# Gated scan chained to the convolution by 16 turns instead of 19, in a twelve-sublayer decoder kernel

## Chip, core and metric

The kernel runs on one core of one Trainium2 chip. The metric is the device time of one launch in microseconds. The three runs of the kernel before gave 3713.7, 3722.3 and 3728.1 us, median 3722.31. The profiled execution is another run.

## What is computed

A decoder of four layers with three sublayers each, every sublayer followed by a residual sum and a layer norm: `x = layernorm(x + f(x))`. x is 128 sequences of 64 positions and 128 features in float32 (8192 tokens). Two neighbouring sublayers matter here, the third of layer 2 and the first of layer 3:

```python
def L2_ffn(x):                         # "convolution with experts"
    xc = causal_depthwise_conv(x, 3 taps) + dw_bias
    x1 = x + silu(xc @ pw_w.T + pw_b)
    logits = x1 @ router_w.T + router_b              # 8 experts, top 2, softmax over the two
    ye = silu(einsum(x1, expert_w) + expert_b)       # all 8 experts
    h = rmsnorm(x1 + (sum_e rw_e * ye_e) @ out_w.T + out_b) * norm_w
    return h + gelu(h @ ff_down_w.T + ff_down_b) @ ff_up_w.T + ff_up_b

def L3_attn(x):                        # "gated scan"
    xn = x / max(|x|, 1e-12) * sqrt(128) * gamma
    q, kv, a = split(xn @ W_qkva.T, 3);  a = sigmoid(a)
    h[t] = a[t] * h[t-1] + kv[t]                     # along the 64 positions
    return q * h
```

## The kernel before

Both x (token rows, `x_tok`) and its transpose (`x_T`) stay on chip through the whole kernel. A sublayer works on 16 chunks of 512 tokens (4 tiles of 128). The engines are programmed by hand, each with its own instruction order, and meet at semaphores.

Sublayers 9 and 10 of the list are chained (`chained`, L1933): one block runs both. On every engine the function `staged` (L1905) goes through turns i = -5, -4, ...; in each turn it calls the stages of the convolution in a fixed order and then those of the scan. A stage with lag l works on chunk i - l, if there is such a chunk. For the scan's stages the offset, 19, is added to the lag. So in turn i TensorE does, in this order, for the convolution: down product (chunk i-4), transposes of the combined experts (i-1), pointwise product, router, experts (i+1), transposes of h (i-3), the z product (i-2), up product (i-5), transposes of the normalised rows (i-7); and then for the scan: `turn_out` (lag 1), `project` (lag -1), `turn_rows` (lag -2), `turn_normed` (lag 3). ScalarE does GELU (i-4), normalise_z (i-3), copy_combined (i-1), copy_h (i-3), square (i-2), normalise (i-6), copy_transposed (i-7), and then scale_rows (-3), sigmoid (-1), copy_turned (-2), normalise_act (2), copy_transposed (3). VectorE does its routing, `combine` (i), `mean_square` (i-2), `residual` (i-5), and then the scan's `residual` (1), `scan` (0), `sum_squares` (-4). GpSimd does squares, powers and sums beside them. An instruction that waits holds up all that stands behind it on its engine.

The eight banks of PSUM all belong to the convolution: pw, route, experts0, experts1, turned, z, down_ps, up_ps. The scan takes them over as they come free. In `project` (L2367) three products of 512 columns are made for a chunk: gate a, then kv, then q. Before, a goes to route, q to experts0 or z, and kv to experts1 or down_ps, by the chunk's parity; the transposed output goes to up_ps, the transposed rows to turned. `scan` (L2442) reads the gate (sigmoid of a, in SBUF) and kv's bank, then multiplies by q's bank into `out_T`, semaphore out_done. `project(c)` waits for the sigmoid of chunk c-1 and for out_done of chunk c-2:

```python
def project(c):                       # L2367
    pe.wait_ge(xs_copied, c + 1)
    if c >= 1:
        pe.wait_ge(gated, c)
    if c >= 2:
        pe.wait_ge(out_done, c - 1)
```

RowTail (L554) is the layer norm of both: the sum and its moments on VectorE, the inverse deviation on GpSimd, normalisation on ScalarE, transposes on TensorE (L637), a copy into x_T on ScalarE (L644). Its row buffer has two places: the residual of chunk c waits until chunk c-2 is normalised (`tail.normed`, L2460). In the profile the digits of names are left out: L2_ffn is L_ffn, L3_attn is L_attn; PSUM banks keep the convolution's names in the scan too. After the scan's last copy a barrier follows, and then the attention "full".

Of the kernel before, what the change touches and what calls it, by code (L numbers as in the profile page):

```python
# [16 lines left out]
N_SUBLAYERS = tuple(range(1, 13))  # L17

ALU = mybir.AluOpType
ACT = mybir.ActivationFunctionType  # L20
# [7 lines left out]
B, S, D = 128, 64, 128  # L28
# [4 lines left out]
CHUNKS = TOKENS // CHUNK  # L33
# [277 lines left out]
class Sublayer:  # L311
# [25 lines left out]
    def bank(self, what):  # L337
        return self.ctx.enter_context(self.nc.psum_tensor(f"{self.name}_{what}", [128, 512], F32))
# [1985 lines left out]
def gated_scan(net, final, name):  # L2324
# [5 lines left out]
    before = yield  # L2330
    with ExitStack() as ctx:
# [8 lines left out]
        if before:  # L2340
            xs_bank, a_bank = before.part["pw"], before.part["route"]
            q_bank, kv_bank = [before.part["experts0"], before.part["z"]], [before.part["experts1"], before.part["down_ps"]]
            y_bank, xT_bank = before.part["up_ps"], before.part["turned"]
        else:
            xs_bank, a_bank = bank("xsT"), bank("a")
            q_bank, kv_bank = [bank("q0"), bank("q1")], [bank("kv0"), bank("kv1")]
            y_bank, xT_bank = bank("y"), bank("xT")
        rooted = sem("gamma_rooted")
# [7 lines left out]
        def tensor(pe):  # L2356
            def turn_rows(c):
                if before and c == 0:
                    pe.wait_ge(before.part["pw_done"], CHUNKS)
                pe.wait_ge(scaled, c + 1)  # L2360
                if c >= 1:
                    pe.wait_ge(xs_copied, c)
                for k in range(PER):
                    last = pe.transpose(xs_bank[:, TILE * k:TILE * k + TILE], xs[:, c % 2, k, :], net.ident[:, :])
                last.then_inc(xs_turned, 1)
# [4 lines that stand above are left out]
                    pe.wait_ge(gated, c)  # L2370
                if c >= 2:
                    pe.wait_ge(out_done, c - 1)
                if c == 0:
                    sub.await_weights(pe)
                if before and c == 0:
                    pe.wait_ge(before.part["r_steps"], before.part["n_steps"]["logits", CHUNKS - 1])
                    pe.wait_ge(before.part["expert_done"], 2 * TILES)
                if before and c == 1:
                    pe.wait_ge(before.part["squared"], CHUNKS)
                    pe.wait_ge(before.part["zn_done"], CHUNKS)  # L2380
                    pe.wait_ge(before.part["down_done"], CHUNKS)
                for r, b in ((2, a_bank), (1, kv_bank[c % 2]), (0, q_bank[c % 2])):
                    pe.matmul(b[:, :], w_s[:, D * r:D * r + D], xn_T[:, c % 2, :], start=True, stop=True)\
                        .then_inc(projected, 1)

            def turn_out(c):
                pe.wait_ge(out_done, c + 1)
                if c >= 1:
                    pe.wait_ge(tail.summed, c)
                if before and c == 0:  # L2390
                    pe.wait_ge(before.tail.summed, CHUNKS)
                for k in range(PER):
                    last = pe.transpose(y_bank[:, D * k:D * k + D], out[:, c % 2, TILE * k:TILE * k + TILE], net.ident[:, :])
                last.then_inc(y_ready, 1)

            def turn_normed(c):
                if before and c == 0 and not final:
                    pe.wait_ge(before.tail.xT_copied, CHUNKS)
                tail.transpose(pe, c, xT_bank)

            return [(1, turn_out), (-1, project), (-2, turn_rows), (3, turn_normed)]

        def scalar(act):
# [19 lines left out]
            def sigmoid(c):  # L2423
                act.wait_ge(projected, 3 * c + 1)
                if c >= 2:
                    act.wait_ge(scanned, c - 1)
                act.activation(gate[:, c % 2, :], a_bank[:, :], ACT.Sigmoid).then_inc(gated, 1)

# [3 lines left out]
        def vector(dve):  # L2432
# [9 lines left out]
            def scan(c):  # L2442
# [4 lines left out]
                dve.wait_ge(projected, 3 * c + 2)  # L2447
                dve.tensor_tensor_scan(h[:, p, :], gate[:, p, :], kv_bank[p][:, :], 0.0, ALU.mult, ALU.add)\
# [5 lines left out]
                dve.tensor_tensor(out[:, p, :], q_bank[p][:, :], h[:, p, :], ALU.mult).then_inc(out_done, 1)  # L2454

# [390 lines left out]
def conv_moe(net, final, name):  # L2846
# [30 lines left out]
    before = yield  # L2877
    with ExitStack() as ctx:
# [333 lines left out]
        def gpsimd(pool):  # L3212
# [43 lines left out]
            "z": z_bank, "down_ps": down_bank, "up_ps": up_bank, "pw_done": pw_done, "r_steps": r_steps, "n_steps": n_steps,  # L3256
            "expert_done": expert_done, "squared": squared, "zn_done": zn_done, "down_done": down_done})

# [37 lines left out]
def build_program(nc, dram):  # L3296
    with ExitStack() as ctx:
# [39 lines left out]
        def run(n, final):  # L3337
# [105 lines left out]
```

## Time and profile before

| | us |
|---|---|
| profiled execution | 3718.39 |
| its span | 3716.7 |
| median of the three runs | 3722.31 |
| TensorE busy | 2948.5 (79% of the span) |
| VectorE busy | 2177.6 (59%) |
| ScalarE busy | 1822.5 (49%) |
| GpSimd busy | 1823.2 (49%) |

Times within the profile are microseconds from the start of the span. The chained stage runs from about 2600 to 3038 us. Busy shares are averages over stages with different limits, and TensorE's clock is granted at one of two levels, so a busy TensorE may be one at half clock (0.50 in the column for the clock).

### The profile page before, as it was taken

The numbers are of one execution on the slowest core, as the hardware profiler recorded it, in microseconds if no ns is written. First come the engines' busy times: TensorE is split into PE (matmuls) and PEld (weight loads), VectorE is DVE, ScalarE is ACT, GpSimd is POOL, SyncE is SP. The second block draws the span as 40 slices with busy tenths as digits, with TensorE's granted clock in tenths as the row PEclk, the third lists the DMA queues.
The fourth block names the chain that finished last, engine by engine and source line by source line (L and its number), as shares of the span: only waits on it lengthen the run. The fifth ranks groups of instructions, "written<-read, shape, count | busy, mean of one in ns | idle before, by whom it ended". The sixth has DMA issues, their size and how long they took to land. (4 is left out here: it accounts for less than half of the span.)

```text
span 3716.7 us, 83881 instructions
## 1 busy us (share of the span) xinstructions
PE 2948.5 (79%) x28814; PEld 2037.6 (55%) x28814; DVE 2177.6 (59%) x5986; ACT 1822.5 (49%) x3516; POOL 1823.2 (49%) x1735
## 2 busy tenths in 40 slices
PE   2687873998888789963529997996999879995884
PEld 1576762775555556642316664664444546664773
DVE  2111133756888668863247886777898668883124
ACT  0233331844555556621216665775466666661332
POOL 3533264434777645526455554663133655553325
PEclk9988986999998889985559998997999789996997
DMA  8555652120010121114621112221000012213664
GB/s 282 160 180 168 193 164 68 45 8 25 32 43 37 41 74 69 71 46 127 168 54 44 55 54 87 87 85 54 1 1 1 4 26 66 73 62 107 198 204 135
DMA packets 325001, 315.46 MB, mean 85 GB/s; under 512 B 111316, under 2 KB 244854, under 8 KB 324473
## 3 DMA queue, kind: packets, MB, share of 16 engines
q1 hardware_dynamic: 283080, 261.98, 23.0%
q0 software_dynamic: 16384, 33.59, 3.0%
q10 hardware_dynamic: 25264, 16.40, 1.5%
q8 instruction: 154, 2.52, 0.3%
q14 instruction: 119, 0.97, 0.1%
HBM read 167.28 MB, written 60.69 MB: 61 GB/s over the span
## 5 line engine op out<-in xcount | busy, mean ns | idle before, releaser
L1099 ACT ACTIVATE moe_first_hid<-moe_first_hid_ps,moe_first_expert_w 128x256 f32<-128x256 f32 x340 | 139.1, 471 | 253.8 <-PE moe_first_hid_ps L1044 132.7
L1055 PE MATMUL moe_first_out_ps<-moe_first_expert_w,moe_first_hid 128*128 128x128 f32 x1360 | 203.0, 304 | 69.0 <-ACT moe_first_hid L1099 45.6
L908 DVE TENSOR_TENSOR moe_first_tile_y<-moe_first_out_ps,moe_first_expert_w 128x256 f32<-128x256 f32 x85 | 36.1, 424 | 374.2 <-PE moe_first_out_ps L1055 213.7
L1055 PEld LDWEIGHTS moe_first_out_ps<-moe_first_expert_w,moe_first_hid 128*128 128x128 f32 x1360 | 184.7, 209 | 81.7 <-issue 39.9
L1118 POOL DMA_INDIRECT slot_x<-x_tok,moe_first_slots x128 | 124.3, 971 | 121.2 <-DMA slot_x<-blank 50.0
L1044 PE MATMUL moe_first_hid_ps<-moe_first_tile_xT,moe_first_expert_w 128*128 128x256 f32 x680 | 174.1, 402 | 2.5 <-issue 1.9
L1132 POOL DMA_INDIRECT moe_first_token_y<-slot_y,moe_first_slots x128 | 123.1, 962 | 107.1 <-issue 66.4
L1814 POOL TENSOR_TENSOR causal_k_blocks<-causal_k_T,headmask 128x1024 f32<-128x1024 f32 x64 | 121.2, 1896 | 99.6 <-PE causal_scores L1424 93.8
L1814 POOL TENSOR_TENSOR alibi_k_blocks<-alibi_k_T,headmask 128x1024 f32<-128x1024 f32 x64 | 121.2, 1896 | 94.2 <-PE alibi_scores L1424 90.1
L1814 POOL TENSOR_TENSOR full_k_blocks<-full_k_T,headmask 128x1024 f32<-128x1024 f32 x64 | 120.7, 1896 | 83.9 <-PE full_scores L1424 78.9
L1099 ACT ACTIVATE moe_last_hid<-moe_last_hid_ps,moe_last_expert_w 128x256 f32<-128x256 f32 x212 | 86.7, 471 | 146.9 <-PE moe_last_hid_ps L1044 110.9
L3072 PE MATMUL L_ffn_experts<-weights_odd,x_T 128*128 128x512 f32 x256 | 145.5, 651 | 1.3 <-ACT L_ffn_expert_out L3168 1.3
L1044 PEld LDWEIGHTS moe_first_hid_ps<-moe_first_tile_xT,moe_first_expert_w 128*128 128x128 f32 x680 | 132.8, 206 | 19.7 <-issue 3.2
L1814 POOL TENSOR_TENSOR keys_k_blocks<-keys_k_T,headmask 128x1024 f32<-128x1024 f32 x64 | 120.9, 1899 | 45.8 <-PE keys_scores L1424 42.1
L908 DVE TENSOR_TENSOR moe_last_tile_y<-moe_last_out_ps,moe_last_expert_w 128x256 f32<-128x256 f32 x53 | 22.5, 424 | 193.1 <-PE moe_last_out_ps L1055 151.2
L2997 DVE SCALAR_TENSOR_TENSOR L_ffn_combined<-L_ffn_expert_out,L_ffn_mix,L_ffn_combined 128x128 f32<-128x128 f32 x448 | 128.7, 350 | 4.0
L1055 PE MATMUL moe_last_out_ps<-moe_last_expert_w,moe_last_hid 128*128 128x128 f32 x848 | 120.9, 296 | 10.4 <-ACT moe_last_hid L1099 7.5
L1814 POOL TENSOR_TENSOR diff_k_blocks<-diff_k_T,headmask 128x1024 f32<-128x1024 f32 x64 | 121.4, 1909 | 10.0 <-POOL diff_k_T L1801 5.6
L3233 POOL TENSOR_SCALAR L_ffn_ms_eps<-L_ffn_ms 128x4 f32<-128x4 f32 x16 | 3.7, 230 | 243.6 <-DVE L_ffn_ms L3005 243.6
L1055 PEld LDWEIGHTS moe_last_out_ps<-moe_last_expert_w,moe_last_hid 128*128 128x128 f32 x848 | 110.9, 203 | 16.4 <-DVE moe_last_tile_y L908 6.3
L1671 DVE TENSOR_REDUCE keys_maxima<-keys_scores 128x8 f32<-128x512 f32 x128 | 87.7, 685 | 49.6 <-PE keys_scores L1424 48.6
L1568 ACT ACTIVATE diff_probs_T<-diff_pT 128x512 f32<-128x512 f32 x128 | 76.1, 595 | 78.9 <-PE diff_pT L1438 78.5
(561 smaller groups left out, 8931.2 us busy)
## 6 DMA issues: line engine op xcount, KB each, us to landing
moe_first_expert_w<-in_L_attn_experts SPq DMA_DIRECT2D x85, 578.0 KB
moe_last_expert_w<-in_L_ffn_experts SPq DMA_DIRECT2D x53, 578.0 KB
moe_first_tile_x<-slot_x SPq DMA_DIRECT2D x85, 128.0 KB
slot_y<-moe_first_tile_y SPq DMA_DIRECT2D x85, 128.0 KB
slot_x<-blank ACTq DMA_DIRECT2D x2, 4992.0 KB, 36.5
L_ffn_tile_x<-slot_x SPq DMA_DIRECT2D x32, 256.0 KB
slot_y<-L_ffn_tile_y SPq DMA_DIRECT2D x32, 256.0 KB
moe_last_tile_x<-slot_x SPq DMA_DIRECT2D x53, 128.0 KB
```

The source lines that it names most:

```text
L908: dve.tensor_tensor(y_out[:, q, :, :], out_bank[q][:, 0:SLOT_TILE].rearrange("p (s d) -> p s d", s=SPAN), over(wall[:, j % RING, 2 * FF + ...
L1044: last = pe.matmul(hid_bank[h][:, SLOT_TILE * (b % 2):SLOT_TILE * (b % 2) + SLOT_TILE], wall[:, j % RING, 128 * b:128 * b + 128], xT[:, j ...
L1055: last = pe.matmul(out_bank[j % 2][:, D * s:D * s + D], hid[:, j % 2, b, TILE * s:TILE * s + TILE], wall[:, j % RING, FF + D * b:FF + D * ...
L1099: act.activation(hid[:, j % 2, b, :], hid_bank[b // 2][:, SLOT_TILE * (b % 2):SLOT_TILE * (b % 2) + SLOT_TILE], gelu, bias=wall[:, j % RIN ...
L1118: pool.indirect_dma_start(slot_x[part][:, :], bass.IndirectOffsetOnAxis(slots[:, part, r, t:t + 1], 0), net.x_tok[:, origin[part] + t, :], ...
L1132: pool.indirect_dma_start(y_in[:, p, k, r, :], None, slot_y[part][0:NTS[part] * SLOT_TILE, :], bass.IndirectOffsetOnAxis(slots[:, part, r, ...
L1568: act.activation(probs_T[:, t.p, 4 * g:4 * g + 4, :].rearrange("p k t -> p (k t)"), pT_bank[:, :], ACT.Copy)\
L1671: dve.tensor_reduce(maxima[:, t.p, heads], src, AX_X, ALU.max).then_inc(max_done, 1)
L1814: pool.tensor_tensor(k_blocks[:, t.p, :, :], keys.to_broadcast([128, 8, TILE]), lanes.to_broadcast([128, 8, TILE]), ALU.mult).then_inc(spr ...
L2997: last = dve.scalar_tensor_tensor(combined[:, p, k, :], expert_out[:, p, k, e, :], w, combined[:, p, k, :], ALU.mult, ALU.add)
L3072: pe.matmul(expert_bank[g][:, :], net.x_T[:, TILE * t:TILE * t + TILE], experts_s[:, 4 * g:4 * g + 4, :].rearrange("p e d -> p (e d)"), st ...
L3233: pool.tensor_scalar(ms_eps[:, :], ms[:, :], 1.0 / D, 1e-6, ALU.mult, ALU.add).then_inc(ms_eps_done, 1)
```

## The change

The offset is 16. The banks are assigned anew: the gate goes to experts0 for chunks 0 to 4 and to down_ps after, q to experts0 (from chunk 6 on odd chunks to up_ps), kv to experts1 (from chunk 8 on odd chunks to turned), the transposed output to route, the transposed rows to z. Where a chunk's q or kv bank is that of the chunk before, `project` waits for out_done of the chunk before; where the gate and q share a bank, the q product waits for the sigmoid. The waits for the convolution's last use of each bank move to the chunk that first takes it.

```diff
         if before:
-            xs_bank, a_bank = before.part["pw"], before.part["route"]
-            q_bank, kv_bank = [before.part["experts0"], before.part["z"]], [before.part["experts1"], before.part["down_ps"]]
-            y_bank, xT_bank = before.part["up_ps"], before.part["turned"]
+            xs_bank, y_bank, xT_bank = before.part["pw"], before.part["route"], before.part["z"]
+            a_banks = [before.part["experts0"] if c < 5 else before.part["down_ps"] for c in range(CHUNKS)]
+            q_banks = [before.part["up_ps"] if c % 2 and c >= 6 else before.part["experts0"] for c in range(CHUNKS)]
+            kv_banks = [before.part["turned"] if c % 2 and c >= 8 else before.part["experts1"] for c in range(CHUNKS)]
...
                 if c >= 2:
                     pe.wait_ge(out_done, c - 1)
+                if c >= 1 and (q_banks[c] is q_banks[c - 1] or kv_banks[c] is kv_banks[c - 1]):
+                    pe.wait_ge(out_done, c)
                 if c == 0:
                     sub.await_weights(pe)
                 if before and c == 0:
-                    pe.wait_ge(before.part["r_steps"], before.part["n_steps"]["logits", CHUNKS - 1])
                     pe.wait_ge(before.part["expert_done"], 2 * TILES)
-                if before and c == 1:
-                    pe.wait_ge(before.part["squared"], CHUNKS)
-                    pe.wait_ge(before.part["zn_done"], CHUNKS)
+                if before and c == 5:
                     pe.wait_ge(before.part["down_done"], CHUNKS)
-                for r, b in ((2, a_bank), (1, kv_bank[c % 2]), (0, q_bank[c % 2])):
-                    pe.matmul(b[:, :], w_s[:, D * r:D * r + D], xn_T[:, c % 2, :], start=True, stop=True)\
-                        .then_inc(projected, 1)
+                if before and c == 7:
+                    pe.wait_ge(before.tail.summed, CHUNKS)
+                if before and c == 9:
+                    pe.wait_ge(before.part["combT_copied"], CHUNKS)
+                    pe.wait_ge(before.part["hT_copied"], CHUNKS)
+                    pe.wait_ge(before.tail.xT_copied, CHUNKS)
+                pe.matmul(a_banks[c][:, :], w_s[:, 2 * D:3 * D], xn_T[:, c % 2, :], start=True, stop=True).then_inc(projected, 1)
+                pe.matmul(kv_banks[c][:, :], w_s[:, D:2 * D], xn_T[:, c % 2, :], start=True, stop=True).then_inc(projected, 1)
+                if a_banks[c] is q_banks[c]:
+                    pe.wait_ge(gated, c + 1)
+                pe.matmul(q_banks[c][:, :], w_s[:, 0:D], xn_T[:, c % 2, :], start=True, stop=True).then_inc(projected, 1)
...
                 if before and c == 0:
-                    pe.wait_ge(before.tail.summed, CHUNKS)
+                    pe.wait_ge(before.part["r_steps"], before.part["n_steps"]["logits", CHUNKS - 1])
...
                 if before and c == 0 and not final:
-                    pe.wait_ge(before.tail.xT_copied, CHUNKS)
+                    pe.wait_ge(before.part["squared"], CHUNKS)
+                    pe.wait_ge(before.part["zn_done"], CHUNKS)
...
-                return chained(net, [conv_moe(net, False, "L2_ffn"), gated_scan(net, N_SUBLAYERS[-1] == 10, "L3_attn")], 19)
+                return chained(net, [conv_moe(net, False, "L2_ffn"), gated_scan(net, N_SUBLAYERS[-1] == 10, "L3_attn")], 16)
```

## Rows read from the trace of the kernel before

**Rows 1.** Windows: length, busy us (instructions) of each engine, TensorE's granted clock, DMA.

```profile
core 0: us, PE busy (x) PEld busy (x) DVE busy (x) ACT busy (x) POOL busy (x), PEclk, DMA share, GB/s
2892.50:2895.00 2.50, 0.25 (x3) 0.28 (x4) 2.46 (x4) 2.15 (x6) 2.42 (x3) 1.00 0.00 0
2895.00:2905.00 10.00, 10.00 (x40) 8.13 (x38) 9.79 (x30) 2.82 (x6) 1.31 (x2) 0.51 0.00 0
...
2895.00:2940.00 45.00, 40.18 (x147) 28.16 (x145) 18.80 (x64) 19.89 (x50) 24.18 (x33) 0.58 0.00 1
...
2953.20:3024.10 70.90, 57.04 (x248) 32.97 (x248) 63.73 (x198) 61.57 (x151) 47.85 (x82) 1.00 0.04 6
```

**Rows 2.** Groups by line, VectorE, 2960 to 3010: count, busy us, mean ns, idle before.

```profile
L580 DVE BATCH_NORM_STATS2 L_attn_ln_stats<-L_attn_resid_sum 128x6 f32<-128x128 f32 x40 | 8.7, 281 | 0.3
...
L2461 DVE TENSOR_TENSOR L_attn_resid_sum<-L_ffn_up_ps,x_tok 128x512 f32<-128x512 f32 x10 | 6.9, 692 | 2.7 <-ACT x_tok L612 2.5
...
L2435 DVE TENSOR_REDUCE L_attn_ss<-L_attn_sq 128x4 f32<-128x512 f32 x10 | 6.7, 674 | 0.0
...
L2448 DVE TENSOR_TENSOR_SCAN L_attn_h<-L_attn_gate,L_ffn_down_ps 128x512 f32<-128x512 f32 x5 | 6.1, 1221 | 0.2
...
L584 DVE BATCH_NORM_AGGREGATE L_attn_ln_moments<-L_attn_ln_stats 128x2 f32<-128x6 f32 x40 | 3.8, 157 | 0.3
...
L2454 DVE TENSOR_TENSOR L_attn_out_T<-L_ffn_z,L_attn_h 128x512 f32<-128x512 f32 x5 | 3.5, 691 | 0.2
```

**Rows 3.** Timeline, TensorE: start, length, instruction, count, idle before and its releaser.

```profile
2860.61 0.39 PE L3096 MATMUL L_ffn_z<-ident,x_T 128*128 128x128 f32 x2
...
2864.73 1.13 PE L3072 MATMUL L_ffn_experts<-weights_odd,x_T 128*128 128x512 f32 x2
...
2910.35 0.63 PE L3096 MATMUL L_ffn_z<-ident,x_T 128*128 128x128 f32 x2
...
2917.55 1.91 PE L3123 MATMUL L_ffn_up_ps<-weights_odd,L_ffn_down 32*128 32x128 f32 x8
...
2924.16 0.66 PE L3109 MATMUL L_ffn_turned<-ident,L_ffn_z_normed 128*128 128x128 f32 x4 [1.81 <-ACT L_ffn_z_normed L3146]
```

**Rows 4.** The tile out_T on VectorE: count, shortest/median/longest ns, first and last start.

```profile
L2454 DVE TENSOR_TENSOR L_attn_out_T<-L_ffn_experts,L_attn_h x8: 691/691/692, 2950.6 to 3023.4; 128x512 f32<-128x512 f32 x8
L2454 DVE TENSOR_TENSOR L_attn_out_T<-L_ffn_z,L_attn_h x8: 691/691/692, 2957.6 to 3028.2; 128x512 f32<-128x512 f32 x8
```

**Rows 5.** Groups by line, ScalarE, 2960 to 3010.

```profile
L612 ACT ACTIVATE x_tok<-L_attn_resid_sum,L_attn_ln_shift,L_attn_ln_rstd 128x128 f32<-128x128 f32 x40 | 16.4, 483 | 0.0
...
L2413 ACT ACTIVATE L_attn_xs<-x_tok,L_attn_inv 128x128 f32<-128x128 f32 x40 | 12.8, 390 | 5.5 <-POOL L_attn_inv L2480 5.5
...
L2421 ACT ACTIVATE L_attn_xn_T<-L_ffn_pw,L_attn_gamma_root 128x512 f32<-128x512 f32 x10 | 6.9, 686 | 0.5
```

**Rows 6.** Timeline, TensorE, one turn of the scan alone.

```profile
2978.81 0.66 PE L2393 MATMUL L_ffn_up_ps<-ident,L_attn_out_T 128*128 128x128 f32 x4 [1.18 <-DVE L_attn_out_T L2454]
...
2979.30 1.02 PE L2383 MATMUL L_ffn_route<-L_attn_xn_T,weights_even 128*128 128x512 f32 x2
...
2981.88 0.60 PE L2364 MATMUL L_ffn_pw<-ident,L_attn_xs 128*128 128x128 f32 x4
```

**Rows 7.** Timeline, TensorE, the first projection.

```profile
2940.87 1.91 PE L2383 MATMUL L_ffn_route<-L_attn_xn_T,weights_even 128*128 128x512 f32 x2
...
2944.53 0.60 PE L2364 MATMUL L_ffn_pw<-ident,L_attn_xs 128*128 128x128 f32 x4
```

**Rows 8.** Timeline, ScalarE: a normalisation, and the table loads of turns 18 and 19.

```profile
2923.01 1.09 ACT L3146 ACTIVATE L_ffn_z_normed<-L_ffn_z,L_ffn_rms_inv 128x128 f32<-128x128 f32 x4
...
2942.89 1.28 ACT L2427 ACT_TABLE_LOAD   x1
...
2944.19 0.60 ACT L2427 ACTIVATE L_attn_gate<-L_ffn_route 128x512 f32<-128x512 f32 x1
...
2945.88 1.28 ACT L3205 ACT_TABLE_LOAD   x1
...
2947.17 0.69 ACT L3205 ACTIVATE L_ffn_down<-L_ffn_down_ps,weights_odd 32x512 f32<-32x512 f32 x1
```

More of the change, by code:

```diff
@@ L2340, in gated_scan @@
         if before:
-            xs_bank, a_bank = before.part["pw"], before.part["route"]
-            q_bank, kv_bank = [before.part["experts0"], before.part["z"]], [before.part["experts1"], before.part["down_ps"]]
-            y_bank, xT_bank = before.part["up_ps"], before.part["turned"]
-        else:
-            xs_bank, a_bank = bank("xsT"), bank("a")
-            q_bank, kv_bank = [bank("q0"), bank("q1")], [bank("kv0"), bank("kv1")]
-            y_bank, xT_bank = bank("y"), bank("xT")
+            xs_bank, y_bank, xT_bank = before.part["pw"], before.part["route"], before.part["z"]
+            a_banks = [before.part["experts0"] if c < 5 else before.part["down_ps"] for c in range(CHUNKS)]
+            q_banks = [before.part["up_ps"] if c % 2 and c >= 6 else before.part["experts0"] for c in range(CHUNKS)]
+            kv_banks = [before.part["turned"] if c % 2 and c >= 8 else before.part["experts1"] for c in range(CHUNKS)]
+        else:
+            xs_bank, y_bank, xT_bank = bank("xsT"), bank("y"), bank("xT")
+            a_banks = [bank("a")] * CHUNKS
+            q_banks, kv_banks = [bank("q0"), bank("q1")] * (CHUNKS // 2), [bank("kv0"), bank("kv1")] * (CHUNKS // 2)
         rooted = sem("gamma_rooted")
@@ L2426, in sigmoid @@
                     act.wait_ge(scanned, c - 1)
-                act.activation(gate[:, c % 2, :], a_bank[:, :], ACT.Sigmoid).then_inc(gated, 1)
+                act.activation(gate[:, c % 2, :], a_banks[c][:, :], ACT.Sigmoid).then_inc(gated, 1)
             return [(-3, scale_rows), (-1, sigmoid), (-2, copy_turned), (2, lambda c: tail.normalise_act(act, c)),
@@ L2447, in scan @@
                 dve.wait_ge(projected, 3 * c + 2)
-                dve.tensor_tensor_scan(h[:, p, :], gate[:, p, :], kv_bank[p][:, :], 0.0, ALU.mult, ALU.add)\
+                dve.tensor_tensor_scan(h[:, p, :], gate[:, p, :], kv_banks[c][:, :], 0.0, ALU.mult, ALU.add)\
                     .then_inc(scanned, 1)
@@ L2453, in scan @@
                     dve.wait_ge(y_ready, c - 1)
-                dve.tensor_tensor(out[:, p, :], q_bank[p][:, :], h[:, p, :], ALU.mult).then_inc(out_done, 1)
+                dve.tensor_tensor(out[:, p, :], q_banks[c][:, :], h[:, p, :], ALU.mult).then_inc(out_done, 1)
             def residual(c):
@@ L3256, in conv_moe @@
             "z": z_bank, "down_ps": down_bank, "up_ps": up_bank, "pw_done": pw_done, "r_steps": r_steps, "n_steps": n_steps,
-            "expert_done": expert_done, "squared": squared, "zn_done": zn_done, "down_done": down_done})
+            "expert_done": expert_done, "combT_copied": combT_copied, "hT_copied": hT_copied, "squared": squared, "zn_done": zn_done, "down_done": down_done})
 def constants():
```

## Prediction, made before the changed kernel was run

> **What bounds the kernel now.** The change lies in one stage, the chained sublayers "convolution with experts" (L2_ffn, shown as L_ffn) and "gated scan" (L3_attn, shown as L_attn), so I read windows of that stage first, then the groups by line of its last part, then the timelines of single engines. A turn is one pass i of the loop in `staged`; the convolution's stage with lag l works in turn i on chunk i - l, the scan's on chunk i - l - offset.
>
> The stage has two regimes. From 2953.2 to 3024.1 us the scan is nearly alone: 70.9 us for 14 chunks, 5.06 us each, VectorE busy 63.7 of 70.9 us, the clock full [rows 1]. There VectorE's own work per chunk is 0.69 + 0.87 + 0.38 (residual and moments) + 1.22 + 0.69 (scan, product) + 0.67 (sum of squares) and small ones, 4.8 us [rows 2], so VectorE bounds it. From 2895 to 2940 (turns 15 to 18) it is the other way round: VectorE busy 18.8 of 45 us, TensorE 40.2, at a mean clock of 0.58 [rows 1]. A turn there is a chain: the z product, 7.2 us at the half clock against 4.1 at the full one, the up product, transposes and the down product, GELU and normalisation on ScalarE, while TensorE waits 1.81 us, and the next z product [rows 3]. The 16 products "out" end at 2951.3, 2958.3 and then one per 5.04 us until 3028.9 [rows 4]; call their ends out(0) to out(15). What follows out(15) is the same in both kernels, so the change is worth what out(15) moves.
>
> **The change part by part.**
>
> *Offset 16 for 19.* Each scan stage runs 3 turns earlier; no instruction goes away. If the three turns saved are scan turns and their work fits into VectorE's idle time, that is 3 x 5.06 = 15.2 us.
>
> *Before turn 15.* Two row scalings (4 x 0.39, next start after 1.2 us) and a copy of 0.69 [rows 5], with gamma's root (about 0.2 us, my estimate from its one column, like the smallest instructions), now stand on ScalarE before the GELU of turn 15: 3.3 us on the path to turn 15's z product, since TensorE already waits for ScalarE there (0.25 us busy in 2.5 us [rows 1]). VectorE's three sums of squares (0.85 each) lie where it waits for ScalarE's tanh, GpSimd's squares and powers where it idles: nothing; if that cover were gone, 3 us.
>
> *The new wait.* For c = 1 to 8 one of project(c)'s banks is that of c - 1, so project(c) waits for out(c-1), which VectorE makes in the same turn. Behind it in TensorE's queue stand turn_rows, the scan's turn_normed and all of the next turn's convolution products. In a turn without convolution this closes a ring: out(c-1), project(c) 2.58 us, turn_rows 0.5 [rows 6], ScalarE copy_turned 0.69 and behind it normalise_act 1.64 [rows 5], for which VectorE's residual waits (it must not overwrite a row buffer not yet normalised), residual 1.94 and scan 2.0 [rows 2]: 9.5 us with 0.2 of hand-overs, against 5.06. And TensorE idles some 5 us in each such ring. After 2.25 us without work in 2.5 the clock stood at 0.51 [rows 1], and the first projection after a pause took 3.66 us instead of 2.58 [rows 7]. I take 3.66, nearest to what happens here: 10.6 us a turn. Bounds: 2.58 (the clock stays up) and 5.1 (three pairs at 1.71 each, all at half clock [rows 7]).
>
> *Sigmoid inside the convolution's tail.* Sigmoid and GELU alternate in turns 15 to 19 instead of 18 and 19: 10 table loads for 4, each 1.28 us and each after the wait of its activation: the load starts 0.1 us after the gate's matmul [rows 8]. For c below 5 the q matmul also waits for the sigmoid, since it writes a's bank. So project(c) costs a 1.9, load 1.28, sigmoid 0.6, q 0.86: 4.7 us, all on the path. The row shows the next activation 0.02 us behind the load. The Trainium skill, "ScalarE: Activation LUTs", What ACT_TABLE_LOAD costs, adds a drain of about 1380 ns to each switch; no idle time of that size stands behind the load here. By that price the sum would be some 8 us higher.
>
> *The sum, as ends of "out".* Turns 15 and 16: z(13) starts at 2895.2 + 3.5 = 2898.7; z 7.2, up and transposes 2.9, project(0) 4.7, turn_rows 0.5, down 1.0, load and GELU 1.96, normalisation 1.09 [rows 8] and copy 0.6, transposes 0.5: z(14) starts at 2919.2; z 7.2, up 1.9, residual 1.95, scan 2.0: out(0) at 2932.4, 18.9 earlier than now. Down is a pair 512 wide like the gate product, up is taken at half its 1.91 us where the clock is full [rows 3, 6]. From there each turn is a chain, because VectorE's scan stands behind the convolution's residual, that behind the up product, that on TensorE behind transposes that wait for ScalarE, and that behind GELU, which needs the down product queued behind project(c):
> - turn 17: project(1) 4.8, turn_rows 0.5, down 1.0, load and GELU 1.96, normalisation 1.09, transposes 0.5, z(15) 6.7, up 1.9, two residuals 3.9, scan 2.0, hand-overs 0.3: 24.6, out(1) at 2957.0 (-1.3).
> - turn 18: the same without z and with up at 1.0: 16.9, out(2) at 2973.9 (+10.7).
> - turn 19: project(3) 4.75, turn_rows 0.45, down 1.0, up 1.0, residuals 3.9, scan 2.0: 13.1, out(3) at 2987.0 (+18.5).
> - turn 20: without down, with the scan's own transposes: 12.7, out(4) at 2999.7 (+26.2).
> - turns 21 to 24: out(5) to out(8) at 10.6 each, the last at 3042.1 against 2993.6: +48.5.
> From project(9) on the banks are double and the pace is 5.06 again. So the sum is +48.5 us, with +28 for the same chains at the full clock (project 3.7, z 4.1, ring 9.5) and about +60 with all projections at half clock. The next sublayer's weights, which SP issues after the last copy of the convolution, still start some 60 us before they are used. GpSimd has at most 9.5 us of work in a turn of 16.9: hidden.
>
> The profiled execution took 3718.4 us (span 3716.7 and 1.7 around it), 3.9 below the median of 3722.3. 3718.4 + 48.5 = 3766.9, from the median 3770.8; I say 3769.
>
> **The rivals.**
> *The clock stays up* (0.2): the added projections keep TensorE busy enough, and only the chains cost: +28, 3750. For it: the clock is full through the scan turns, with TensorE busy only 57.0 of 70.9 us [rows 1]. Against it: those gaps are 0.7 to 1.2 us [rows 6], the new ones 3 to 5. TensorE was busy 10.00 of 10 us from 2895 to 2905 and stayed at 0.51 [rows 1]. The Trainium skill, "TensorE: Matmul & The Clock Gate", Part 1, says that the throttled state is the default and activity releases it; the trace does not agree for the z product, which is busy time alone. By that rule the z products would run at full clock too, and it is this rival.
>
> *Even* (0.12): the turns shared with the convolution cost nothing net, as the steps of its chain overlap more than I see, and only the four pure rings pay: 4 x (9.5 - 5.06) = 17.8 against 15.2 saved: 3725. For it: VectorE idles 26 of 45 us [rows 1]. Against it: it idles because it waits in its queue for the up product, and the scan stands behind that.
>
> *Faster* (0.08): project(c) finds out(c-1) done, because TensorE arrives at it later than VectorE leaves it. Then the wait is free and 15.2 us are kept: 3707. It decides by the idle time before project(c) in turns 17 to 24: under 0.5 us each it holds. Against it: in the turns now, TensorE goes on with project(c) 0.5 us after turn_out starts [rows 6], some 4 us before the same turn's scan is through.
>
> The forecast has 0.6. A measurement of this kernel can tell about 0.5% (18.6 us) from no change. Slower by more than that: 0.6 + 0.2 = 0.8; within: 0.12; faster: 0.08 (3707 would hardly reach it, but a further gain by a clock kept up would add to it). The range leaves out the two last cases, goes down to +10 for a clock partly up and chains partly overlapped, and up to +66 for the half-clock bound and dearer loads: 3732 to 3788.
>
> **What would show it.** Right: TensorE's idle time before project(c), released by the product "out", of 3 to 5 us in turns 17 to 24 and none from c = 9; ten table loads between the last SILU and the end of the stage; out(0) some 19 us earlier than now and out(8) some 48 later; ScalarE idle before the sigmoid in these turns; a clock near 0.5 for most of 2895 to 3040; turns of 10 to 11 us for c = 5 to 8. Wrong: scan turns near 5 us for c = 5 to 8 (the ring is not closed), or out(1) 10 or more us earlier than now (the clock is up). If the stage's end moves by less than 10 us, the chain is not what orders the shared turns.

## Result and the profile after

The changed kernel took 3780.27 us (median of 4 runs, 3778.8 to 3784.94), the kernel before 3725.2 us in the runs beside it (4 runs, 3713.7 to 3736.69): a ratio of 1.0151, 95% interval 1.0124 to 1.0177. The forecast was 3769 us, slower. The profiled execution took 3779.84 us with a span of 3778.2.

The spans of the two profiled executions differ by more than the stage does, so the stage is measured by itself: from the first instruction of the convolution to the first load of the next sublayer. In the kernel before that is 2580.6 to 3039.3 us, 458.7 us. Two rows of the tile views give it for the changed kernel (count, shortest/median/longest ns, first and last start):

```profile
L2939 DVE TENSOR_SCALAR L_ffn_conv<-x_T,weights_odd x16: 399/536/548, 2595.0 to 2826.6; 128x512 f32<-128x512 f32 x16
...
L1315 SPq DMA_DIRECT2D full_xT_in<-x_T x16: 497/520/632, 3105.6 to 3362.8; - x16
```

2595.0 to 3105.6 is 510.6 us: +51.9, against a forecast of +48.5. The spans differ by 61.5: another 14.4 us were there before the stage began (5.6 of it at the first load of the diff attention, far ahead of the change), and 4.8 came back behind it.

The windows of the changed kernel answer to [rows 1]; its stage began 14.4 us later than that of before.

```profile
core 0: us, PE busy (x) PEld busy (x) DVE busy (x) ACT busy (x) POOL busy (x), PEclk, DMA share, GB/s
2910.00:2955.00 45.00, 34.80 (x114) 21.98 (x112) 21.10 (x58) 22.82 (x47) 22.46 (x27) 0.66 0.00 1
2955.00:3010.00 55.00, 33.41 (x134) 20.28 (x134) 23.05 (x83) 32.26 (x68) 25.45 (x40) 0.75 0.00 1
3010.00:3060.00 50.00, 28.82 (x94) 15.56 (x94) 21.20 (x66) 23.99 (x60) 18.26 (x32) 0.80 0.05 7
3060.00:3095.00 35.00, 25.30 (x112) 14.74 (x112) 30.06 (x93) 26.53 (x64) 17.97 (x34) 0.97 0.00 1
```

From 3010 to 3060 us, turns of the scan nearly alone (some normalisations and transposes of the convolution's last chunks are still in them), VectorE is busy 21.2 of 50 us, where it was busy 63.7 of 70.9 [rows 1]. From 3060 on, with two banks in turn, it is busy 30.1 of 35 again. The table of waits, 2890 to 3060 us (total, times, longest), names what came instead:

```profile
DVE L_attn_resid_sum L2470 <- ACT x_tok L612: 28.0, 4, 7.7
...
PE L_ffn_down_ps L2388 <- DVE L_attn_out_T L2463: 21.5, 4, 5.7
...
PE L_ffn_experts L2388 <- DVE L_attn_out_T L2463: 17.1, 4, 5.1
```

TensorE waits eight times, 38.6 us in all, for the product "out" ahead of project: the eight chunks with the new wait. VectorE waits four times, 28.0 us, for ScalarE to empty a row buffer: the other half of the ring in the four turns without convolution. One such ring, c = 7, first on TensorE, then VectorE, then ScalarE (timelines):

```profile
3036.48 2.05 PE L2388 MATMUL L_ffn_down_ps<-L_attn_xn_T,weights_even 128*128 128x512 f32 x2 [5.35 <-DVE L_attn_out_T L2463]
3038.32 1.91 PE L2389 MATMUL L_ffn_experts<-L_attn_xn_T,weights_even 128*128 128x512 f32 x2
3040.03 1.84 PE L2392 MATMUL L_ffn_up_ps<-L_attn_xn_T,weights_even 128*128 128x512 f32 x2
3041.70 0.60 PE L2365 MATMUL L_ffn_pw<-ident,L_attn_xs 128*128 128x128 f32 x4
...
3048.85 2.04 PE L2388 MATMUL L_ffn_down_ps<-L_attn_xn_T,weights_even 128*128 128x512 f32 x2 [5.68 <-DVE L_attn_out_T L2463]
```

```profile
3035.54 0.69 DVE L2463 TENSOR_TENSOR L_attn_out_T<-L_ffn_experts,L_attn_h 128x512 f32<-128x512 f32 x1
...
3044.69 0.69 DVE L2470 TENSOR_TENSOR L_attn_resid_sum<-L_ffn_route,x_tok 128x512 f32<-128x512 f32 x1 [7.66 <-ACT x_tok L612]
...
3046.76 1.22 DVE L2457 TENSOR_TENSOR_SCAN L_attn_h<-L_attn_gate,L_ffn_experts 128x512 f32<-128x512 f32 x1
3048.01 0.69 DVE L2463 TENSOR_TENSOR L_attn_out_T<-L_ffn_up_ps,L_attn_h 128x512 f32<-128x512 f32 x1
```

```profile
3042.34 0.69 ACT L2430 ACTIVATE L_attn_xn_T<-L_ffn_pw,L_attn_gamma_root 128x512 f32<-128x512 f32 x1 [3.18 <-PE L_ffn_pw L2365]
3042.92 1.63 ACT L612 ACTIVATE x_tok<-L_attn_resid_sum,L_attn_ln_shift,L_attn_ln_rstd 128x128 f32<-128x128 f32 x4
```

Read as one chain: out(6) ends 3036.23; 0.25 later project(7) starts and takes 5.22, all at the half clock; turn_rows 0.64, copy_turned 0.58, normalise_act 1.77 (each to the start of the next), residual and moments 2.07, scan and product 1.94. That is 12.47 us, where a turn took 5.04 before [rows 4].

ScalarE's table loads (timeline) answer to [rows 8]. Here and below a turn ends with its product out, as in the forecast's sum (turn 17 with out(1)); these are from turns 16 and 17:

```profile
2946.93 1.28 ACT L2436 ACT_TABLE_LOAD   x1
2950.36 0.60 ACT L2436 ACTIVATE L_attn_gate<-L_ffn_experts 128x512 f32<-128x512 f32 x1 [2.14 <-PE L_ffn_experts L2388]
2953.86 0.69 ACT L2430 ACTIVATE L_attn_xn_T<-L_ffn_pw,L_attn_gamma_root 128x512 f32<-128x512 f32 x1 [2.91 <-PE L_ffn_pw L2365]
2954.57 1.28 ACT L3214 ACT_TABLE_LOAD   x1
2955.86 0.68 ACT L3214 ACTIVATE L_ffn_down<-L_ffn_down_ps,weights_odd 32x512 f32<-32x512 f32 x1
```

The sigmoid's load starts 3.4 us ahead of the sigmoid, right behind scale_rows and within the idle time. GELU's load, right behind copy_turned, has no such cover.

### The profile page after: what moved, and what is told of

Same layout as the page of the kernel before. It is cut to its first block and busy times, and to the rows that moved or that the text cites. A ratio compares the mean times of both kernels' runs of the same rounds, so it can differ in the third digit from the quotient of the medians.

```text
span 3778.2 us, 83894 instructions
## 1 busy us (share of the span) xinstructions
PE 2968.1 (79%) x28814; PEld 2043.9 (54%) x28814; DVE 2184.0 (58%) x5986; ACT 1829.0 (48%) x3522; POOL 1826.0 (48%) x1735
## 5 line engine op out<-in xcount | busy, mean ns | idle before, releaser
L1044 PEld LDWEIGHTS moe_first_hid_ps<-moe_first_tile_xT,moe_first_expert_w 128*128 128x128 f32 x680 | 132.3, 205 | 18.9 <-issue 2.6
L3006 DVE SCALAR_TENSOR_TENSOR L_ffn_combined<-L_ffn_expert_out,L_ffn_mix,L_ffn_combined 128x128 f32<-128x128 f32 x448 | 136.3, 367 | 4.0
L1671 DVE TENSOR_REDUCE diff_maxima<-diff_scores 128x8 f32<-128x512 f32 x128 | 87.2, 681 | 52.7 <-PE diff_scores L1424 52.7
```

The costliest lines, as they stand in the source:

```text
L1044: last = pe.matmul(hid_bank[h][:, SLOT_TILE * (b % 2):SLOT_TILE * (b % 2) + SLOT_TILE], wall[:, j % RING, 128 * b:128 * b + 128], xT[:, j ...
L1671: dve.tensor_reduce(maxima[:, t.p, heads], src, AX_X, ALU.max).then_inc(max_done, 1)
L3006: last = dve.scalar_tensor_tensor(combined[:, p, k, :], expert_out[:, p, k, e, :], w, combined[:, p, k, :], ALU.mult, ALU.add)
```

## The experiments

The first two rows are the kernels above. The control and e1 to e7 ran on two other chips, where the kernel before has medians of 3573.15 and 3573.38 us; e8 to e11 ran where it has 3724.0. Each ratio is against the kernel before on the same chip. The stage repeats far better than the whole: before's is 458.7 us in both of its profiles. So each kernel is compared by its stage and by the ends of "out", in us from the first convolution instruction (start of the row on L2463, or its like, + 0.69). Stage and ends are from one profile of each kernel; the ratio is of the times, with its 95% interval. The intervals reach 6 to 15 us to either side, so a difference of a few us between two stages rests on single profiles. It can also be the clock of one product: the z product of turn 15 took 7.2 us in before, e1 and e2, but 4.0 in e6 and e10, though these two have no products added. From the transposes of h to the up product that is 4.5 us in e6, 7.6 in before (TensorE's timeline of e6):

```profile
2779.36 0.63 PE L3112 MATMUL L_ffn_turned<-ident,L_ffn_z_normed 128*128 128x128 f32 x4 [2.64 <-ACT L_ffn_z_normed L3149]
...
2783.86 1.05 PE L3126 MATMUL L_ffn_up_ps<-weights_odd,L_ffn_down 32*128 32x128 f32 x8
```

| kernel | offset | stage | out(0) | out(4) | out(8) | out(15) | ratio |
|---|---|---|---|---|---|---|---|
| before | 19 | 458.7 | 370.7 | 392.9 | 413.1 | 448.3 | 1 |
| changed | 16 | 510.6 | 353.1 | 417.8 | 465.0 | 500.2 | 1.0151 [1.0124, 1.0177] |
| e1_offset19 | 19 | 513.9 | 371.9 | 420.2 | 468.3 | 503.4 | 1.0158 [1.0117, 1.0198] |
| e2_scan_first | 16 | 469.8 | 332.8 | 398.6 | 425.4 | 458.5 | 1.0033 [1.0014, 1.0052] |
| e3_rows_first | 16 | 493.6 | 348.3 | 410.4 | 449.4 | 483.1 | 1.0114 [1.0076, 1.0152] |
| e4_gate_without_table | 16 | 508.1 | 349.8 | 414.8 | 462.5 | 497.6 | 1.0179 [1.0162, 1.0197] |
| e5_fill_after | 16 | 492.3 | 342.3 | 404.3 | 445.0 | 481.8 | 1.0109 [1.0092, 1.0126] |
| e7_fill_before | 19 | 455.2 | 364.5 | 389.4 | 409.7 | 444.8 | 1.0004 [0.9988, 1.0020] |
| e6_before_scan_first | 19 | 456.9 | 364.3 | 393.0 | 412.7 | 445.6 | 1.0007 [0.9991, 1.0023] |
| e8_scan_before_residual | 16 | 486.1 | 353.5 | 417.5 | 443.3 | 474.8 | 1.0073 [1.0048, 1.0097] |
| e9_scan_first_fill | 16 | 458.7 | 333.9 | 387.6 | 414.3 | 447.4 | 1.0013 [0.9989, 1.0037] |
| e10_scan_first_19 | 19 | 465.2 | 369.4 | 400.2 | 421.2 | 453.9 | 0.9994 [0.9972, 1.0016] |
| e11_before_both | 19 | 451.7 | 362.1 | 387.9 | 407.6 | 440.4 | 0.9978 [0.9956, 1.0000] |

**ctl_before: the kernel before once more.**

> The kernel before, unchanged, for a second trace. In the two traces at hand the convolution stage begins at 2580.6 us (before) and at 2595.0 (after), though nothing is changed ahead of it. If that is a difference between executions, the stage may begin anywhere from 2575 to 2600 here and its own length (first convolution instruction to the first load of the next attention, 458.7 us before, 510.6 after) repeats within 2 us. If the change moved what lies ahead, this trace begins the stage at 2581 within 3 us.

One run, 3563.85 us. The stage began at 2460.3 us instead of 2580.6 and took 458.7 us again, as expected. On this faster chip its start cannot tell where the 14.4 us ahead of the stage come from.

**e1_offset19: banks and wait of the change, offset of before.**

```diff
-... gated_scan(net, N_SUBLAYERS[-1] == 10, "L3_attn")], 16)
+... gated_scan(net, N_SUBLAYERS[-1] == 10, "L3_attn")], 19)
```

> The changed kernel with the offset back at 19: single banks and the new wait, but almost no sharing of turns. My theory (the wait closes a ring of out, project, turn_rows, copy_turned, normalise_act, residual, scan) gives eight rings of 11 to 12 us in place of 5.06: about +50 us against the kernel before, 3775, with the clock falling in each ring. The rival (the loss comes from sharing turns with the convolution's tail: table loads, long chains) gives a time within 10 us of the kernel before, 3725.

+55.2 us: banks and wait alone cost as much as the whole change (the intervals of the two ratios overlap). The ends of "out" are 11.1 to 12.9 us apart from c = 1 to 8, and 5 us from c = 9. The offset by itself brings out(0) 18.8 us forward (353.1 against 371.9), of which 3.3 are left at the end: in the changed kernel the first four turns with the wait share their time with the convolution and take 64.7 us, here 48.3.

**e2_scan_first: VectorE does scan and sum of squares first in a turn.**

```diff
-            staged(joined(flows[0].vector(dve), flows[1].vector(dve)), AHEAD, BEHIND)
+            second = flows[1].vector(dve)
+            early = [(lag + offset, stage) for lag, stage in second if lag <= 0 and scan_first]
+            late = [(lag, stage) for lag, stage in second if lag > 0 or not scan_first]
+            staged(early + joined(flows[0].vector(dve), late), AHEAD, BEHIND)
```

> The changed kernel, but VectorE does the scan and the sum of squares at the start of a turn, ahead of the convolution's stages and of the scan's residual. My theory: the product out(c-1) is then done before TensorE comes to project(c), the ring is open and the clock stays up: rings of 11.7 us fall to about 5 (4 x 6.5 = 26 us) and the shared turns 16 to 20 lose waits of 3 to 5 us each, 20 to 35 us in all: 3715 to 3735. If the wait for the bank is not the cause but the table loads and the clock in the shared turns, it gains 10 us at most: 3770.

40.8 of the 51.9 us are gone with wait and offset in place. Timelines of TensorE and VectorE, c = 7 and 8:

```profile
2886.06 1.10 PE L2391 MATMUL L_ffn_down_ps<-L_attn_xn_T,weights_even 128*128 128x512 f32 x2 [2.81 <-DVE L_attn_out_T L2466]
...
2890.79 1.10 PE L2391 MATMUL L_ffn_down_ps<-L_attn_xn_T,weights_even 128*128 128x512 f32 x2 [0.61 <-DVE L_attn_out_T L2466]
```

```profile
2886.63 0.69 DVE L2473 TENSOR_TENSOR L_attn_resid_sum<-L_ffn_route,x_tok 128x512 f32<-128x512 f32 x1
...
2888.70 1.22 DVE L2460 TENSOR_TENSOR_SCAN L_attn_h<-L_attn_gate,L_ffn_experts 128x512 f32<-128x512 f32 x1
```

The residual follows the product and has its buffer free; the projection starts 4.7 us after the one before. The wait is still there, yet from c = 7 on the pace is VectorE's own again (out(5) and out(6) still follow after 9.0 and 7.8 us).

**e3_rows_first: the ring cut elsewhere.** turn_rows goes ahead of project on TensorE, copy_turned and normalise_act ahead of the sigmoid on ScalarE.

```diff
-            return [(1, turn_out), (-1, project), (-2, turn_rows), (3, turn_normed)]
+            return [(1, turn_out), (-2, turn_rows), (-1, project), (3, turn_normed)]
```

> The changed kernel, with turn_rows ahead of project on TensorE, and copy_turned and normalise_act ahead of the sigmoid on ScalarE. The wait is the same, but row turning and normalisation no longer stand behind it. My theory: the ring is then out, gate product, sigmoid, scan, some 5 us, with the residual beside it: the rings of chunks 5 to 8 fall from 11.7 to 6 or less (-22 us or more), the shared turns hardly change since the down product still stands behind project: about 3752. A rival by which the sigmoid or the gate's product is the late link: within 8 us of the changed kernel, 3780.

The stage is 17.0 us shorter than the changed kernel's, 7.4 of it by out(4), where hardly any had been expected. But the rings of c = 5 to 8 still take 8.4 to 11.4 us, more than this cut had promised. What is late now (waits for the tile of the residual, then TensorE's timeline):

```profile
its engine sat idle before it (us, times) until:
  PE L_ffn_route L2401: 23.3, 8
```

```profile
2903.61 1.02 PE L2392 MATMUL L_ffn_up_ps<-L_attn_xn_T,weights_even 128*128 128x512 f32 x2
2904.47 0.60 PE L637 MATMUL L_ffn_z<-ident,x_tok 128*128 128x128 f32 x4
2904.91 0.60 PE L2401 MATMUL L_ffn_route<-ident,L_attn_out_T 128*128 128x128 f32 x4
```

The residual now waits for turn_out, which stands in TensorE's queue behind the three products held by the wait. The ring has two ways back to VectorE; this edit cut one.

**e4_gate_without_table: what the table loads cost.** It leaves out the sigmoid of chunks 0 to 4.

```diff
-                act.activation(gate[:, c % 2, :], a_banks[c][:, :], ACT.Sigmoid).then_inc(gated, 1)
+                act.activation(gate[:, c % 2, :], a_banks[c][:, :], ACT.Sigmoid if c >= 5 else ACT.Identity).then_inc(gated, 1)
```

> The changed kernel, with the gate of chunks 0 to 4 computed by ScalarE's Identity instead of Sigmoid (so the sigmoid of these five chunks is left out), which leaves one load of a table in the shared turns instead of alternating ones. It takes apart the price of the table loads from the rest of the ring. The prediction's step: each of ten loads of 1.28 us stands after the wait of its activation and lies on the path, so with eight gone the stage (first convolution to the next sublayer's first load) becomes 10 us shorter than the 510.6 us of the changed kernel: 499 to 501. Theory from the trace after: the sigmoid's loads run before the wait for the gate's product and only the GELU's, right behind the copy of the turned rows, hold the path up, so four to five times 1.28 us: 504 to 506. Rival: no load is on the path, the ring through VectorE sets the pace alone: 510 to 511. In all three the rings of chunks 5 to 8 keep their 11 to 12.5 us.

The stage is 2.5 us shorter than the changed kernel's, between the theory's 504 to 506 us and the rival's 510 to 511. Turns 15 to 20 have two table loads instead of ten. By out(0) 3.3 us are gained, by out(2) 4.3, and 1.0 is given back in turn 19. Timelines of ScalarE, then TensorE:

```profile
2842.28 0.69 ACT L2430 ACTIVATE L_attn_xn_T<-L_ffn_pw,L_attn_gamma_root 128x512 f32<-128x512 f32 x1 [3.18 <-PE L_ffn_pw L2365]
2843.26 0.68 ACT L3214 ACTIVATE L_ffn_down<-L_ffn_down_ps,weights_odd 32x512 f32<-32x512 f32 x1 [0.29 <-PE L_ffn_down_ps L3125]
```

```profile
2852.89 2.04 PE L2388 MATMUL L_ffn_experts<-L_attn_xn_T,weights_even 128*128 128x512 f32 x2 [5.14 <-DVE L_attn_out_T L2463]
...
2856.43 1.91 PE L2392 MATMUL L_ffn_experts<-L_attn_xn_T,weights_even 128*128 128x512 f32 x2
```

GELU starts 0.98 us after copy_turned instead of 2.00: the load is worth 1.0 us here and not 1.28, since without it GELU waits 0.29 us for the down product. In turn 19 the idle time before project(3) is 5.14 us instead of 4.26 and its third product takes 1.91 instead of 1.28: there the clock takes some of the gain back. The whole time cannot be told from the changed kernel's (the intervals overlap).

**e5_fill_after: what the clock costs.** Products of 384 columns that nobody reads fill TensorE's idle time.

```diff
+                if 1 <= c <= 8:
+                    fill(pe, (3, 4, 4)[c - 1] if c < 4 else 5, c + 1)
```

(and three ahead of turn_h in turn 15, two in turns 16 to 18)

> The changed kernel with products of 384 columns added on TensorE that nobody reads, into a bank that stands idle: three ahead of the transposes of h in turn 15, two in turns 16 to 18, and three to five ahead of the wait for the product out in the projections of chunks 1 to 8. They fill the time in which TensorE would wait, so they show what the granted clock is worth. The prediction put 20 us on the half clock (48.5 at the mixed clock against 28 at full). If it is right the granted clock stands near 1.0 in the ring and the stage falls from 510.6 us to 488 to 496, each ring of chunks 5 to 8 to about 9.5 to 10.3 us. Rival: the ring is set by ScalarE, VectorE and fixed latencies, the half clock costs nothing, or the added products cost what they give: 508 to 516.

18.3 us shorter. The first window answers to 2910:2955 in the changed kernel (clock 0.66), the second reaches from out(4) to out(8), as 3012.8:3060 there (0.80); behind them a ring at full clock, c = 8:

```profile
core 0: us, PE busy (x) PEld busy (x) DVE busy (x) ACT busy (x) POOL busy (x), PEclk, DMA share, GB/s
2794.50:2839.50 45.00, 36.72 (x161) 23.87 (x162) 18.21 (x54) 24.17 (x50) 19.29 (x26) 0.88 0.00 1
2883.80:2924.50 40.70, 32.72 (x124) 18.57 (x124) 18.60 (x58) 22.85 (x56) 15.88 (x27) 0.96 0.06 9
```

```profile
2909.24 3.46 PE L2364 MATMUL L_ffn_pw<-weights_even 128*128 128x384 f32 x10
2914.83 1.12 PE L2402 MATMUL L_ffn_down_ps<-L_attn_xn_T,weights_even 128*128 128x512 f32 x2 [2.12 <-DVE L_attn_out_T L2477]
2915.79 1.02 PE L2403 MATMUL L_ffn_experts<-L_attn_xn_T,weights_even 128*128 128x512 f32 x2
2916.65 1.02 PE L2406 MATMUL L_ffn_experts<-L_attn_xn_T,weights_even 128*128 128x512 f32 x2
```

In this ring 3.46 us of added work stand in a gap of 5.6. Projections 7 and 8 take 2.7 us instead of 5.22 and 4.16, and out(7) and out(8) follow 9.7 us after the one before. It does not hold everywhere: behind 3.39 us of added work project(6) still began at half clock and took 4.4 us, and out(6) followed after 11.4. In turn 17 the z product fell to half clock, 6.0 us instead of the changed kernel's 4.0, and out(1) followed after 23.2 us instead of 21.4.

**e7_fill_before: the same in the kernel before**, turns 15 to 18.

> The kernel before with products of 384 columns added on TensorE that nobody reads, three ahead of the transposes of h in turn 15 and two in turns 16 to 18, while TensorE would wait there for ScalarE. The trace of before shows the clock at half in these turns and the z products at 6.7 to 7.2 us instead of 4.1. If the clock is kept up by them, up to 3 us in each of four turns come back: stage 446 to 452 us instead of 458.7, time 0.2 to 0.35 per cent less. Rival: VectorE's convolution or ScalarE's copies set the turn, or the products stand in the way of those that count: 457 to 462.

3.5 us shorter in the stage, which lies between expectation and rival; the whole time cannot be told from before's (0.9988 to 1.0020). TensorE's timeline, turns 16 and 17 (transposes of h, and the up product behind the z product):

```profile
2796.38 1.09 PE L3121 MATMUL L_ffn_turned<-ident,L_ffn_z_normed 128*128 128x128 f32 x4 [1.29 <-ACT L_ffn_z_normed L3158]
...
2804.46 1.91 PE L3135 MATMUL L_ffn_up_ps<-weights_odd,L_ffn_down 32*128 32x128 f32 x8
...
2811.51 0.60 PE L3121 MATMUL L_ffn_turned<-ident,L_ffn_z_normed 128*128 128x128 f32 x4
...
2815.97 1.05 PE L3135 MATMUL L_ffn_up_ps<-weights_odd,L_ffn_down 32*128 32x128 f32 x8
```

Two of three z products run at the full clock (turn 17: 4.46 us from transposes to up, 6.62 in the kernel before; turn 15: 4.49 and 7.62, but there e6 has the same without added products); the one of turn 16 still takes 8.1 us with its transposes. out(0) ends 6.2 us earlier, but out(1) follows 9.7 us later instead of 7.0: ahead of it project(1) now runs at half clock, 4.35 us instead of 2.65.

**e6_before_scan_first: the order alone, in the kernel before.** The edit of e2 without wait and banks.

> The kernel before (offset 19, its own banks, no added wait) with VectorE doing scan and sum of squares of a shared turn ahead of the convolution's stages. It is the control for the same order in the changed kernel, where it took 41 us off. Theory: that gain came from the wait for the product out, which the kernel before does not have, so here only the three shared turns can move: stage 455 to 462 us. Rival: the order by itself is worth much in any kernel: 440 us or less.

1.8 us shorter, with the z product of turn 15 at full clock. So the 40.8 us of e2 are no virtue of the order as such: it pays by what it takes off the wait.

**e8_scan_before_residual: only the two of the scan's own stages exchanged.**

```diff
-            return [(1, residual), (0, scan), (-4, sum_squares)]
+            return [(0, scan), (1, residual), (-4, sum_squares)]
```

> The changed kernel, with one thing exchanged: in VectorE's list of the gated scan the scan of a chunk stands ahead of the residual of the chunk before. The convolution's stages stay first in a shared turn. It takes the last link out of the forecast ring (normalise_act, residual, scan) and leaves the wait, the offset and everything else. Theory (the wait costs as much as it does because the residual's link is in the ring): the rings of chunks 5 to 8, 11.2 to 12.5 us in the changed kernel, fall to between 5 and 9 us, the shared turns 15 to 18 stay within 2 us of the changed kernel's, stage 476 to 488 us instead of 510.6. Rival (most of what the larger exchange took off, 41 us, came from the scan going ahead of the convolution's stages): stage 500 us or more.

24.5 us shorter than the changed kernel, nearly all of it behind out(4) (417.5 against 417.8); the rings of c = 5 to 8 take 5.7, 7.8, 5.8 and 6.5 us. The shared turns did not quite stay within the 2 us expected: out(1) and out(2) came 3.0 and 3.3 us later, as the z product of turn 17 took 7.2 us here and 4.0 in the changed kernel. The other 16.3 us of e2 come with the rest of its edit: the scan ahead of the convolution's stages in the shared turns, and the sum of squares with it. No run takes these two apart.

**e9_scan_first_fill and e10_scan_first_19: can the smaller offset win?** e2 with the added products of turns 15 to 18; and e2 with the offset at 19.

> The changed kernel with scan and sum of squares first on VectorE in each turn (stage 469.8 us by itself) and with the added products of 384 columns ahead of the transposes of h, three in turn 15 and two in turns 16 to 18. The two remedies in one kernel, as the likeliest way for the smaller offset to win. Theory: the products bring back 2 to 3 us in each of the four shared turns, stage 458 to 463 us, the same as before within what can be measured (ratio 0.998 to 1.004). Rival: the shared turns are bound by VectorE's convolution and the clock gives nothing there, 468 to 472 us.

> The changed kernel with scan and sum of squares first on VectorE, and the offset back at 19. Against the same kernel at offset 16 (stage 469.8 us) it shows what the offset alone is worth once the wait is cheap. Theory: the four turns that the smaller offset shares cost more than the three turns it saves, so at 19 the stage is 457 to 464 us, 6 to 13 us shorter. Rival: the offset by itself saves up to the 15 us of three turns as the arithmetic of turns has it, so at 19 the stage is 475 to 485 us.

e9: 458.7 us, 11.1 less than e2 and the same as before. The z products of turns 15, 16 and 17 took 7.2 us each in e2 and 4.0 each here, 9.5 us together. At offset 16 with both remedies the change comes to nothing. e10: 465.2 us, 4.6 less than at offset 16, where 6 to 13 had been expected. With e6 this splits the 11.1 us that e2 still loses: order -1.8, banks and waits +8.3, offset +4.6. The split is rough: the z product of turn 15 took 4.0 us in e10 and 7.2 in e2, so up to 3.2 of the 4.6 may be the clock. What is clear is that the 15.2 us do not appear. Behind the 8.3 stands, likely, the second new wait (no run took it out): at offset 19 the q product of a chunk below 5 waits for the sigmoid, since it writes the gate's bank (four times in e10, 7.9 us in all; TensorE's timeline):

```profile
2957.10 1.12 PE L2395 MATMUL L_ffn_experts<-L_attn_xn_T,weights_even 128*128 128x512 f32 x2 [1.10 <-ACT L_attn_gate L2439]
2966.52 2.07 PE L2395 MATMUL L_ffn_experts<-L_attn_xn_T,weights_even 128*128 128x512 f32 x2 [3.49 <-ACT L_attn_gate L2439]
```

**e11_before_both: e6 and e7 together.**

> The kernel before with both remedies: scan and sum of squares first on VectorE (stage 456.9 us by itself) and the added products (455.2 us by itself). It is the candidate to beat both kernels. Expected, if the two add: stage 452 to 455 us against 458.7, a ratio of 0.998 to 0.9995, at the edge of what a measurement tells. Rival: they take the same idle time, 455 to 457 us.

451.7 us, 7.0 less than before and more than the two by themselves (1.8 and 3.5). The median is 3718.01 us (12 runs) against 3724.0, ratio 0.9978 with an interval that ends at 1.0000: the stage is shorter than in either kernel, the whole time only at the edge of what can be told.

## Why the prediction came out right, step by step

**The wait closes a ring: shown.** Eight waits ahead of project, 3.15 to 5.68 us, none from c = 9. e1 has them without the offset and is as slow; e2 and e8 take VectorE's links out, and 40.8 and 24.5 us of the 51.9 go.

**The size of the ring: 1.2 us too small.** The forecast had 10.6 us for c = 5 to 8, the trace 12.3, 11.2, 12.5 and 11.3. The term that was mis-sized is the projection: 3.66 us assumed, 5.0, 4.05, 5.22 and 4.16 measured. That is 3.8 of the 4.8 us by which the four rings are longer; the rest lies in the other links and the hand-overs. The upper bound of 5.1 was nearer than the value taken.

**The shared turns: right within 1.3 us at out(4).** Ends against the forecast, both as moves against before: out(0) -17.6 (-18.9), out(1) -3.2 (-1.3), out(2) +8.7 (+10.7), out(3) +16.7 (+18.5), out(4) +24.9 (+26.2). Turn 17 took 21.4 us instead of 24.6, because its z and up products ran at the full clock: 5.0 us together, forecast 8.6. TensorE's timeline answers to [rows 3]: 4.53 us from the transposes of h to the up product.

```profile
2957.59 0.66 PE L3118 MATMUL L_ffn_turned<-ident,L_ffn_z_normed 128*128 128x128 f32 x4 [2.79 <-ACT L_ffn_z_normed L3155]
...
2962.12 1.05 PE L3132 MATMUL L_ffn_up_ps<-weights_odd,L_ffn_down 32*128 32x128 f32 x8
```

The z product of turn 15, though, had already moved by 5.7 us against before, where the forecast had 3.5 in its sum (3.3 in its text). So the agreement at out(4) is better than its terms.

**"All ten loads on the path": wrong.** There were ten, but from the second turn on the sigmoid's loads ran ahead of their wait. The forecast took it from [rows 8] that a load starts after the wait of its activation, 0.1 us behind the gate's product. That row cannot show it: ScalarE had only just become free (timeline of before).

```profile
2941.61 1.26 ACT L2413 ACTIVATE L_attn_xs<-x_tok,L_attn_inv 128x128 f32<-128x128 f32 x4
```

Its work ends at 2942.87, and the load starts at 2942.89. In the changed kernel all ten loads start 0.01 to 0.02 us behind the instruction before them. It hardly showed in the sum, as project came out slower by the clock: project(2) took 4.5 us, forecast 4.7, but 4.5 of three products at nearly half clock, not of a load. That two errors met there is luck: with eight of the ten loads gone the stage falls by 2.5 us (e4), where the forecast's prices make 8 x 1.28 = 10.2. GELU's load costs 1.0 us in the turn shown. The Trainium skill, "ScalarE: Activation LUTs", What ACT_TABLE_LOAD costs, adds a drain of about 1380 ns to each switch. The trace does not agree: GELU starts 1.29 us after the start of its 1.28 us load.

**The clock: right in worth, not in the picture.** The forecast put 20.5 us between mixed and full clock; filling the gaps gave 18.3 (20.0 at out(8)). The rival "the clock stays up" falls: it had +28 us, where +51.9 came; with most gaps filled (e5) it is +33.6. But the clock was not near 0.5 for most of the stretch; it went to and fro between its two levels, 0.66 to 0.80 on the mean. The rule of the page "TensorE: Matmul & The Clock Gate" of the Trainium skill, Part 1, that activity releases the throttle, fares better here than I gave it: in e9 the products that nobody reads go with three z products of 4.0 us instead of e2's 7.2. Still, within the z product of turn 16, busy time alone, the clock did not rise in the kernel before or in the changed one (7.2 and 6.8 us).

**The offset saves at most 15.2: it saved far less.** 3.3 us are left of it with the wait (e1), and once the order is mended the profile with it is 4.6 us longer (e2 against e10), of which 3.2 may be the clock of one product. Rival "faster" fell by its own sign: the idle time before project(c) was 3.15 us and more, not under 0.5. "Even" fell because the shared turns cost as much as the rings: 24.9 of 51.9 us stand at out(4).

**Open.** Why the stretch ahead of the stage was 14.4 us longer in the profiled execution was not looked into; nothing is changed there. Such differences also lie between the other traces: the stage starts at 2460.3 to 2479.5 us in the eight of the control and e1 to e7, at 2583.9 to 2597.3 in the four of e8 to e11. Before's own times have a range of 23 us in these 4 runs and of 35.6 in the 35 beside e8 to e11. Open too is how much of a difference of 2 to 5 us between two stages is the clock of a single product.

## What to carry to other kernels

A wait for something made in the same turn closes a ring through every queue it crosses: add up the ring, not the wait. Then see which stages stand in a queue ahead of what the ring needs though they need not; exchanging two entries of a list (e8) brought back 24.5 of 51.9 us, more than the 15.2 us that the smaller offset could have saved at best. Before starting a stage earlier, ask which of its turns will be shared, and whether a shared turn is bound by the same engine: three turns of 5 us saved were paid with four of 13 to 21.

## What the runs showed of the hardware

- Added products, in the ring shown 3.46 us in a gap of 5.6 us, went with a granted clock of 0.96 from out(4) to out(8) where it had been 0.80; project(7) took 2.7 us instead of 5.22, project(6) still 4.4. The stage fell by 18.3 us. In the kernel before, a few in turns 15 to 18 went with a stage 3.5 us shorter, with the order of e6 7.0.
- The z product of turn 15 took 4.0 or 7.2 us in kernels without added products (e6 and e10; before, e1 and e2).
- In turns 15 to 20 of the changed kernel each table load started 0.01 to 0.02 us behind the instruction before it, also where its activation still had to wait (load at 2946.93, wait over at 2950.36). GELU's load, whose activation had almost nothing to wait for, cost 1.0 us of its 1.28.
- The stage of the kernel before repeated to 0.1 us in two traces, on chips where its whole times differ by 4%: what one stage gains is better read from its own length than from the time of the kernel.
